# GpSimd's gathers of a chunk: the waits for the preceding chunk's scores and messages are given up, the wait for the sums stays

## The chip, the cores and the metric

One core of one Trainium2 chip. The metric is the device time of one execution in microseconds. The core has five engines that run their own instruction streams and meet at semaphores: TensorE (PE in the profile, its weight loads PEld), VectorE (DVE), ScalarE (ACT), GpSimd (POOL) and SyncE (SP), which issues transfers.

## What is computed

A graph layer followed by a mixture-of-experts layer, each added to its input. The changed code belongs to the graph layer, whose core is:

```python
h_fwd = h @ W_forward.T            # h: 6250 x 256, normalised rows of x
h_rev = h @ W_reverse.T            # 6250 x 64 each
messages = h_fwd[src] * direction[:, 0:1] + h_rev[src] * direction[:, 1:2]   # 200000 edges
scores = leaky_relu(einsum('ef,hf->eh', messages, attn_forward[0]), 0.2)     # 4 heads
exp_scores = exp(scores - scores.max(axis=0))
sum_exp = segment_sum(exp_scores, dst, N)
norm = exp_scores / (sum_exp[dst] + 1e-10)
out = stack([segment_sum(messages * norm[:, hd:hd+1], dst, N) for hd in range(4)], 1)
```

The edges are sorted by `dst`.

## The kernel before

A first stage makes a table of 6272 rows (`node_table`, in HBM): for each node its forward and reverse products and its attention scores, 136 numbers a row. A second stage, the loop over chunks of edges that this case is about, goes through the 200000 edges in 98 chunks (`NCH`) of 16 sets (`K`) of 128 edges. Two chunks make one pass of the hardware loop, and each tensor that is filled ahead has two slots (`RING`), so slot `s` is that of the chunk's parity. Behind it come the expert layer and the last normalisation, which the change does not touch.

What each engine does for chunk `c`:

- GpSimd gathers the table rows of the edges' sources, one indirect transfer of 128 rows (one set) at a time (L259), 14 sets a chunk (`KG`). It works ahead: while the other engines are at chunk `c-1`, it gathers chunk `c`, into the slot that chunk `c-2` has left.
- The other two sets of a chunk (`FILL`), called hot rows, come from TensorE instead: VectorE builds one-hot matrices in two halves (L1070), TensorE multiplies them with a copy of the table that lies on the chip (`fetch`, L979, 34 matmuls a set), ScalarE takes the first third of the result from PSUM (L940), VectorE adds the other two thirds (L1081). While at chunk `c`, TensorE fetches set 1 of chunk `c+1`, then does chunk `c`'s sums, then fetches set 0 of chunk `c+2`.
- VectorE weights the rows by the edge weights (L1005, L1008, L1011), builds the second half of a one-hot matrix (for which TensorE must be through with the fetch before), forms the raw scores (L1025) and the scores (L1027, which raise `score_ready`), the messages (L1038, `msg_ready`) and, from ScalarE's exponentials, the weighted one-hot windows (L1042, `val_ready`). Later it adds TensorE's window sums to the accumulator (L1000, eight instructions, behind a wait for `summed`).
- TensorE multiplies messages with the weighted windows: 32 matmuls for a chunk's sums (`sum_units`, L876), the last of which raises `summed`.
- SyncE loads the next chunk's indices and weights once a chunk's gathers are complete, and the keys of coming hot rows.

GpSimd issues its instructions in the order in which they are written. The only thing that spaces them are its waits. `piece(a, b)` issues the gathers of sets a to b-1. Semaphores count chunks: `msg_ready` at `c-1` means that chunks 0 to `c-2` have their messages, `summed` at `c-1` that chunks 0 to `c-2` are summed, `score_ready` at `c` and `msg_ready` at `c` that the chunk before this one, `c-1`, has its scores and its messages. `settle` raises a semaphore (`turns`) for which nobody waits; the wait written ahead of it stands at that increment.

Of the kernel before, what the change touches and what calls it, by code (L numbers as in the profile page):

```python
# [46 lines left out]
K = 16  # L47
# [52 lines left out]
def after(eng, sem, count):  # L100

    if isinstance(count, int) and count <= 0:
        return
    eng.wait_ge(sem, count)


def settle(eng, turns):


    eng.sem_inc(turns, 1)  # L110
# [107 lines left out]
def stage_edges(nc, tensors, g):  # L218
# [4 lines left out]
    with ExitStack() as edges:  # L223
# [32 lines left out]
        def gather(pool, s, ks, done):  # L256

            for k in ks:
                pool.indirect_dma_start(out=rows[:, s, k, :], out_offset=None, in_=table,  # L259
                                        in_offset=bass.IndirectOffsetOnAxis(ap=index[:, s, 0, k:k + 1], axis=0))\  # L260
                    .then_inc(done, 16)
# [509 lines left out]
        with ExitStack() as ctx:  # L771
# [21 lines left out]
            turns = sem("pool_turns")  # L793
# [5 lines left out]
            msg_ready = sem("messages_ready")  # L799
            hot_ready = sem("hot_ready")  # L800
            max_taken = sem("max_taken")
            score_ready = sem("score_ready")
# [12 lines left out]
            def chunks(eng, begin, step, begun=0):  # L815


                loaded = begin(0)
                for s in range(begun, RING):
                    step(s, s, 0, loaded)  # L820
                with eng.Fori(1, NIT - 2) as it:
                    loaded = begin(it)
                    for s in range(RING):
                        step(it * RING + s, s, it, loaded)
                for it in range(NIT - 2, NIT):
                    loaded = begin(it)
                    for s in range(RING):
                        step(it * RING + s, s, it, loaded)

            def final(c):  # L830

                return isinstance(c, int) and c == NCH - 1
# [5 lines left out]
            def whole(it):  # L838

                return isinstance(it, int) and it == NIT - 1  # L840
# [55 lines left out]
            @block.gpsimd  # L896
            def _(pool):
                def step(c, s, it, _):
                    pool.wait_ge(index_ready[s], 16 * (it + 1))
                    after(pool, msg_ready, c - RING + 1)  # L900
                    settle(pool, turns)
                    begun = EARLY_SETS if isinstance(c, int) and c == EARLY else 0
                    sets = K_LAST if final(c) else K if whole(it) else KG

                    def piece(a, b):
                        gather(pool, s, range(max(a, begun), min(b, sets)), gathered[s])

                    piece(0, 1)
                    after(pool, summed, c - 1)
                    settle(pool, turns)  # L910
                    piece(1, 7)
                    pool.wait_ge(score_ready, c)
                    settle(pool, turns)
                    piece(7, 11)
                    pool.wait_ge(msg_ready, c)
                    settle(pool, turns)
                    piece(11, K)
                pool.wait_ge(prepared, 1)
                chunks(pool, lambda it: None, step, EARLY)

# [1298 lines left out]
```

## Time and profile before

| | us |
|---|---|
| median of 3 runs | 2936.72 (2936.69 to 2939.57) |
| the profiled execution's own time | 2938.83 |
| its span in the trace | 2937.0 |
| busy: PE / PEld / DVE / ACT / POOL | 2194.4 / 1993.9 / 1797.7 / 432.5 / 1630.8 |
| busy POOL in gathers (L259), 1375 of them | 1303.7 |
| idle of POOL just before gathers | 874.8 |

Busy time counts instructions that do work; waits, register and branch instructions are not in it. A matmul's end is modelled in the trace, so a matmul drawn as ended need not be ended. A gather's row on POOL is the time in which its transfer is issued, and its data arrive later. In the timeline views each row is: start us, duration us, engine, line, operation, what it writes and reads, how many instructions are merged in the row, and in brackets the engine's idle time just before it and what ended that. "issue" there means that the profile shows nothing that it waited for, "remote" that a semaphore came whose sender the profile does not name.

### The profile page before, as it was taken

What the parts mean: (1) busy time and instruction counts of PE and PEld (TensorE: products, weight loads), DVE (VectorE), ACT (ScalarE), POOL (GpSimd) and SP (SyncE); (2) the same over time, 40 slices, a digit from 0 to 9 for tenths busy, and PEclk for the clock granted to TensorE, in tenths of its full rate; (3) what the DMA queues carried; (4) which work ended last, traced back from release to release, by engine and by line L of the source; (5) the groups of instructions that cost most, each with busy time, mean ns of one, the idle gap of its engine ahead of it and who ended that gap; (6) DMA issues with size and microseconds to landing.
All of it is one profiled execution on the core that took longest, in us unless ns stands there. A gap on an engine that the chain in (4) does not pass through costs nothing.

```text
span 2937.0 us, 48035 instructions
## 1 busy us (share of the span) xinstructions
PE 2194.4 (75%) x13105; PEld 1993.9 (68%) x13106; DVE 1797.7 (61%) x4481; ACT 432.5 (15%) x1222; POOL 1630.8 (56%) x1750
## 2 busy tenths in 40 slices
PE   6577877778787777787777777777873547999990
PEld 6476767767677676677677677676763446888880
DVE  6666665666565566566556566665654566666666
ACT  4000000000000000000000000000001432434344
POOL 6565565565665555656655656655653555333326
PEclk8789898898898898888888888988985558999995
DMA  5222222222222222222222222222223456556557
GB/s 184 52 53 49 51 51 50 51 52 50 50 53 50 49 51 50 51 48 53 52 48 51 52 50 52 52 50 49 54 48 121 137 174 186 200 187 206 192 170 264
DMA packets 176306, 256.67 MB, mean 87 GB/s; under 512 B 47079, under 2 KB 121000, under 8 KB 176005
## 3 DMA queue, kind: packets, MB, share of 16 engines
q0 software_dynamic: 53696, 121.60, 16.6%
q1 hardware_dynamic: 122564, 134.56, 14.9%
q8 instruction: 17, 0.28, 0.0%
q14 instruction: 29, 0.23, 0.0%
HBM read 218.11 MB, written 38.79 MB: 87 GB/s over the span
## 4 chain that ended last, share of the span: by engine, by line
DVE 29%; issue 26%; PE 24%; another core or an unknown queue 11%; DVEq 7%; DMA 2%; POOL 1%; ACT 1%; SPq 0%; ACTq 0%; POOLq 0%
PE p_hot L979 18%; DVE onehot L1070 5%; DVE shared L1000 3%; DVEq L1726 3%; DVE hot_ex L1042 2%; PE p_win L876 2%; DVE p_part L1008 2%; DVE rows L1081 1%; DVE rows L1005 1%; PE p_y L1894 1%; DVEq L867 1%; DVE p_y L1949 1%; PE p_h L1884 1%; DVE hot L1019 1%
## 5 line engine op out<-in xcount | busy, mean ns | idle before, releaser
L259 POOL DMA_INDIRECT rows<-node_table,index x1375 | 1303.7, 948 | 874.8 <-issue 470.6
L979 PE MATMUL p_hot<-parts,onehot 128*128 128x408 f32 (+1 forms) x6392 | 1410.1, 379 | 364.6 <-issue 192.8
L979 PEld LDWEIGHTS p_hot<-parts,onehot 128*128 128x128 f32 x6392 | 1288.8, 213 | 473.1 <-issue 263.2
L1070 DVE TENSOR_TENSOR onehot<-key,p_dve 128x1152 fp32r<-128x1152 f32 x376 | 473.8, 1281 | 108.8 <-PE p_hot L979 62.0
L1000 DVE TENSOR_TENSOR shared<-shared,p_win 65x64 f32 x784 | 170.9, 218 | 489.1 <-remote 382.0
L876 PE MATMUL p_win<-hot_ex,msg 128*65 128x64 f32 x3136 | 231.5, 228 | 165.1 <-issue 124.6
L876 PEld LDWEIGHTS p_win<-hot_ex,msg 128*65 128x65 f32 x3136 | 207.0, 142 | 196.8 <-issue 195.3
L940 ACT ACTIVATE rows<-p_hot,third 128x136 f32<-128x136 f32 x188 | 70.5, 375 | 1603.9 <-PE p_hot L979 990.5
L1081 DVE SCALAR_TENSOR_TENSOR rows<-p_hot,third,rows 128x136 f32<-128x136 f32 x376 | 134.9, 359 | 243.5 <-issue 192.3
L1735 POOL DMA_INDIRECT expert_rows<-ys,back x104 | 103.1, 992 | 269.4 <-DVE ys L1954 198.4
L1884 PEld LDWEIGHTS p_h<-xt,shared 128*128 128x128 f32 x1664 | 199.9, 194 | 33.9 <-ACT xt L1826 28.6
L1884 PE MATMUL p_h<-xt,shared 128*128 128x128 f32 x1664 | 212.4, 282 | 7.9 <-ACT xt L1826 5.4
L1894 PE MATMUL p_y<-shared,hid_t 128*128 x832 | 199.1, 383 | 9.3 <-DVE hid_t L1921 8.6
L1894 PEld LDWEIGHTS p_y<-shared,hid_t 128*128 128x128 f32 x832 | 151.3, 192 | 26.7 <-issue 9.9
L1305 POOL DMA_INDIRECT dispatched<-xn,slot_i x98 | 100.8, 1028 | 95.3 <-issue 63.4
L1921 DVE TENSOR_SCALAR hid_t<-p_h,shared 128x128 f32<-128x128 f32 x208 | 63.4, 347 | 123.2 <-PE p_y L1894 72.6
L1005 DVE TENSOR_TENSOR rows<-rows,p_attr 128x1088 f32<-128x1088 f32 x98 | 125.7, 1282 | 10.7 <-DMA rows<-node_table,index 5.8
L1008 DVE TENSOR_TENSOR p_part<-rows,p_attr 128x1024 f32<-128x1024 f32 x98 | 119.6, 1221 | 0.0
L1038 DVE TENSOR_TENSOR msg<-rows,p_part 128x1024 f32<-128x1024 f32 x98 | 118.8, 1212 | 0.0
L1042 DVE TENSOR_TENSOR hot_ex<-hot,p_ex 128x1024 f32<-128x1024 bf16 x98 | 118.8, 1212 | 0.0
L931 ACT ACTIVATE p_ex<-score,neg_shift 128x64 f32<-128x64 f32 x98 | 31.2, 318 | 433.5 <-issue 313.3
L1857 ACT ACTIVATE own<-xs,is_first 128x256 f32<-128x256 f32 x104 | 53.1, 510 | 209.4 <-DVE is_first L1932 191.0
(270 smaller groups left out, 1419.0 us busy)
## 6 DMA issues: line engine op xcount, KB each, us to landing
shared<-in_w SPq DMA_DIRECT2D x120, 512.0 KB
rows<-node_table,index POOLq DMA_INDIRECT x1375
xs<-dispatched SPq DMA_DIRECT2D x104, 129.5 KB
key<-hot_keys SPq DMA_DIRECT2D x94, 128.0 KB
shared<-expert_rows SPq DMA_DIRECT2D x12, 896.0 KB, 7.8
token_rows<-in_x SPq DMA_DIRECT2D x7, 896.0 KB
shared<-in_x SPq DMA_DIRECT2D x7, 768.0 KB
out<-shared SPq DMA_DIRECT2D x6, 896.0 KB, 7.3
```

Source lines behind the costliest of these rows:

```text
L259: pool.indirect_dma_start(out=rows[:, s, k, :], out_offset=None, in_=table, in_offset=bass.IndirectOffsetOnAxis(ap=index[:, s, 0, k:k + 1] ...
L876: last = pe.matmul(psum[0:MSG, u * HEADS * W:(u + 1) * HEADS * W], msg[:, k, :], weighted[:, k, :, :].rearrange("p h w -> p (h w)"), start ...
L979: last = pe.matmul(p_hot[:, j, 0:width * ROW], onehot[:, gr, :], parts[:, gr:NT:GP, m, :], start=(gr == 0 and m == 0), stop=(gr == ORDER[- ...
L1000: return dve.tensor_tensor(to, to, psum.rearrange("p (h w) -> p h w", h=HEADS), ALU.add)
L1005: dve.tensor_tensor(rows[:, s, :, 0:COLS], rows[:, s, :, 0:COLS], attr_p[:, 0, :].unsqueeze(2).broadcast_to([P, K, COLS]), ALU.mult)\
L1008: dve.tensor_tensor(p_part[:, :, :], rows[:, s, :, COLS:COLS + HD], attr_p[:, 1, :].unsqueeze(2).broadcast_to([P, K, HD]), ALU.mult)\
L1038: dve.tensor_tensor(msg[:, :, 0:HD], rows[:, s, :, 0:HD], p_part[:, :, :], ALU.add)\
L1042: dve.tensor_tensor(hot_ex[:, :, :, :], hot[:, :, :].unsqueeze(2).broadcast_to([P, K, HEADS, W]), ex_p.unsqueeze(3).broadcast_to([P, K, HE ...
L1070: dve.tensor_tensor(onehot[:, a:b, :], key[:, s, j, :].unsqueeze(1).broadcast_to([P, b - a, P]), group_p[:, a:b].unsqueeze(2).broadcast_to ...
L1081: dve.scalar_tensor_tensor(out=row, in0=p_hot[:, j, m * ROW:(m + 1) * ROW], scalar=third[:, m, ds(f, 1)], in1=row, op0=ALU.mult, op1=ALU.add)\
L1884: last = pe.matmul(p_h[:, u, f // 2, (f % 2) * P:(f % 2 + 1) * P], w1_r[:, r % R5, c, f * P:(f + 1) * P], xt[:, u, c, :], start=(c == 0), ...
L1894: last = pe.matmul(p_y[:, u, 0:D], hid_t[:, u, c, :], w2_sb[:, ds(e, 1), c, :] .rearrange("p a d -> p (a d)"), start=(c == 0), stop=(c == ...
```

## The change

The two waits inside a chunk's gathers and the two `settle` calls behind them are taken out, and the three last pieces become one. The wait for the index, the wait for the messages of chunk `c-2` ahead of the first gather, and the wait for the sums of chunk `c-2` behind it stay as they were.

```diff
                     piece(0, 1)
                     after(pool, summed, c - 1)
                     settle(pool, turns)
-                    piece(1, 7)
-                    pool.wait_ge(score_ready, c)
-                    settle(pool, turns)
-                    piece(7, 11)
-                    pool.wait_ge(msg_ready, c)
-                    settle(pool, turns)
-                    piece(11, K)
+                    piece(1, K)
```

On GpSimd, in the loop over chunks, one even chunk stood like this before; `rows` is the gathered slot, `node_table` the table, and the names in brackets are the semaphores waited for (`window_summed` is `summed`, `messages_ready` is `msg_ready`):

```order
L259 DMA rows<-node_table,index 128x136 [waits messages_ready]
L259 DMA rows<-node_table,index 128x136 [waits window_summed]
L259 DMA rows<-node_table,index 128x136 x5
L259 DMA rows<-node_table,index 128x136 [waits score_ready]
L259 DMA rows<-node_table,index 128x136 x3
L259 DMA rows<-node_table,index 128x136 [waits messages_ready]
L259 DMA rows<-node_table,index 128x136 x2
```

The same chunk of the changed kernel on GpSimd, with the first two gathers of the odd chunk behind it:

```order
L259 DMA rows<-node_table,index 128x136 [waits messages_ready]
L259 DMA rows<-node_table,index 128x136 [waits window_summed]
L259 DMA rows<-node_table,index 128x136 x12
L259 DMA rows<-node_table,index 128x136 [waits index_ready1,messages_ready]
L259 DMA rows<-node_table,index 128x136 [waits window_summed]
```

The 14 gathers are the same and in the same order; the twelve behind the wait for the sums now follow one another without a wait, up to the first gather of the next chunk. No instruction of another engine moves.

## Rows read from the trace of the kernel before

**Rows 1.** The page, busy time, share of the span and instructions of each engine.

```profile
PE 2194.4 (75%) x13105; PEld 1993.9 (68%) x13106; DVE 1797.7 (61%) x4481; ACT 432.5 (15%) x1222; POOL 1630.8 (56%) x1750
```

**Rows 2.** Line L1005 (durations, first and last start), and what ended its waits.

```profile
L1005 DVE TENSOR_TENSOR rows<-rows,p_attr x98: 1275/1281/1290, 92.9 to 2244.3; 128x1088 f32<-128x1088 f32 x98
...
DMA rows<-node_table,index: 5.8, 1
```

**Rows 3.** Line L259, the gathers: idle time before them by releaser (us, times).

```profile
issue: 470.6, 1243
remote: 223.9, 82
DVE score L1027: 179.7, 48
DVE msg L1038: 0.6, 2
```

**Rows 4.** Timeline of POOL, two chunks from 1000 us.

```profile
1003.33 0.95 POOL L259 DMA_INDIRECT rows<-node_table,index  x1 [2.42 <-remote]
...
1011.71 0.94 POOL L259 DMA_INDIRECT rows<-node_table,index  x1 [1.19 <-issue]
...
1020.45 0.95 POOL L259 DMA_INDIRECT rows<-node_table,index  x1 [0.30 <-issue]
1024.23 0.95 POOL L259 DMA_INDIRECT rows<-node_table,index  x1 [2.83 <-remote]
...
1030.48 0.95 POOL L259 DMA_INDIRECT rows<-node_table,index  x1 [0.30 <-issue]
1035.43 1.00 POOL L259 DMA_INDIRECT rows<-node_table,index  x1 [4.00 <-DVE score L1027]
...
1044.24 0.95 POOL L259 DMA_INDIRECT rows<-node_table,index  x1 [0.30 <-issue]
```

**Rows 5.** Timeline of DVE, the same two chunks.

```profile
1002.68 2.67 DVE L1000 TENSOR_TENSOR shared<-shared,p_win 65x64 f32 x8 [5.41 <-remote]
...
1023.58 2.67 DVE L1000 TENSOR_TENSOR shared<-shared,p_win 65x64 f32 x8 [2.10 <-remote]
...
1034.42 0.23 DVE L1027 SCALAR_TENSOR_TENSOR score<-raw 128x64 f32<-128x64 f32 x1
...
1046.97 2.67 DVE L1000 TENSOR_TENSOR shared<-shared,p_win 65x64 f32 x8 [5.80 <-remote]
```

**Rows 6.** Timeline of PE, the sums of the same two chunks.

```profile
1014.47 2.06 PE L876 MATMUL p_win<-hot_ex,msg 128*65 128x64 f32 x31
...
1038.11 2.10 PE L876 MATMUL p_win<-hot_ex,msg 128*65 128x64 f32 x32 [1.12 <-issue]
```

**Rows 7.** Timeline of ACT, hot rows taken from PSUM in the same chunks.

```profile
1017.61 0.38 ACT L940 ACTIVATE rows<-p_hot,third 128x136 f32<-128x136 f32 x1 [6.34 <-remote]
...
1032.81 0.38 ACT L940 ACTIVATE rows<-p_hot,third 128x136 f32<-128x136 f32 x1 [14.59 <-remote]
```

**Rows 8.** Timelines of DVE, POOL, PE and ACT in a chunk with a late restart.

```profile
956.00 2.66 DVE L1000 TENSOR_TENSOR shared<-shared,p_win 65x64 f32 x8 [5.79 <-remote]
...
979.25 2.67 DVE L1000 TENSOR_TENSOR shared<-shared,p_win 65x64 f32 x8 [3.44 <-remote]
...
959.37 0.94 POOL L259 DMA_INDIRECT rows<-node_table,index  x1 [5.14 <-issue]
...
975.63 0.95 POOL L259 DMA_INDIRECT rows<-node_table,index  x1 [0.30 <-issue]
...
967.74 1.75 PE L876 MATMUL p_win<-hot_ex,msg 128*65 128x64 f32 x26
...
971.94 0.37 ACT L940 ACTIVATE rows<-p_hot,third 128x136 f32<-128x136 f32 x1 [7.34 <-issue]
```

**Rows 9.** Timelines of PE and DVE in the last chunk, after the last gather.

```profile
2250.16 3.75 PE L876 MATMUL p_win<-hot_ex,msg 128*65 128x64 f32 x32 [12.73 <-DVE hot_ex L1042]
...
2254.05 2.65 DVE L1000 TENSOR_TENSOR shared<-shared,p_win 65x64 f32 x8 [3.99 <-PE p_win L876]
```

## The prediction, made before the changed kernel had run

> **What bounds the kernel now.** I began with the page's busy line [rows 1]: no engine is full (PE 75%, DVE 61%, POOL 56% of the span), so the time is made of waits, and the stage with the change has to be read by its waits. That stage is the loop over 98 chunks of edges. The view of line L1005, VectorE's first instruction of each chunk, runs from 92.9 to 2244.3 us [rows 2]: 2151.4 us over 97 periods, 22.18 us a chunk, 73% of the span. The reader should see one more thing in that view: L1005 is the instruction that needs the gathered rows, and in the whole run it waited for a gather once, 5.8 us. The rows that GpSimd fetches are never late. What a quicker GpSimd gives cannot come from there.
>
> Next the waits before the gathers [rows 3]. GpSimd idles 179.7 us for the scores in 48 waits (3.74 us each) and 0.6 us for the messages; the waits put down to "remote" (223.9 us) are largely those for the sums, which stay.
>
> Then two neighbouring chunks in the timeline [rows 4]. After the sums GpSimd issues at a fixed pace, 0.95 us a gather and 0.30 us between two. In the first of the two chunks the score wait stretches one gap to 1.19 us (0.89 too much), in the second to 4.00 us (3.70 too much). The chunks alternate like this through the loop.
>
> Last, who ends the chunk. VectorE starts to add the window sums (L1000) at 1002.68, 1023.58 and 1046.97 us [rows 5]. TensorE's records of the 32 sums say that they were done long before: they start at 1014.47 and at 1038.11 and are drawn 2.1 us long (31 records in the first case, a straggler follows) [rows 6], so VectorE starts 9.1 and 8.9 us after TensorE's first sum. In the last chunk, where GpSimd gathers nothing any more, the same 32 sums start at 2250.16 and L1000 follows at 2254.05, 3.89 us later [rows 9]. So TensorE's results are seen late while gathers run. And the moment is tied to the last gather: that one ends at 1020.45+0.95=1021.40 and L1000 starts 2.18 us later; in the next chunk it ends at 1044.24+0.95=1045.19 and L1000 starts 1.78 us later [rows 4, 5]. By this reading a chunk lasts as long as GpSimd's run of 14 gathers, plus what stands around it, and the pause for the scores lies inside that run.
>
> The rows hold a test of it. In one chunk GpSimd restarts late, 3.37 us after the sums (956.00 to 959.37 us), and therefore finds the scores ready; it issues 14 gathers without a pause and ends at 975.63+0.95=976.58 us. L1000 follows at 979.25, 2.67 us after the last gather [rows 8]. The later run has the later sums behind it. Eleven such chunks stand eight apart.
>
> **The change part by part.**
> (1) *The wait for the messages* goes. It cost 0.6 us in all [rows 3]: nothing.
> (2) *The wait for the scores* goes, in every chunk, with its semaphore increment. GpSimd's own idle time that can vanish is 179.7−48×0.30=165.3 us, plus 0.89 us in some 46 chunks of the other sort, 41 us: 206 us at most [rows 3, 4]. This does not follow through one for one, so I build the new chunk instead.
> (3) *The new period.* From L1000 to the first gather behind it: 1002.68 to 1003.33, 0.65 us. Fourteen gathers without a pause: 959.37 to 976.58, 17.21 us. From their end to L1000: 1.78, 2.18 or 2.67 us; I take 2.67, because it belongs to the only row without a score pause [rows 4, 5, 8]. Sum 20.53 us. The late restart comes every eighth chunk: (3.37−0.65)/8=0.34 us a chunk, which I keep in full. 20.87 us against 22.18: 1.31 us gained.
> (4) *Times the chunks.* The first chunks and the last two (which fetch no hot rows) gain nothing by it; I count 93 periods: 122 us. 2938.83 (the profiled execution's own time) −122=2817; that execution lies 2.1 us above the median of the runs, so **2815 us**.
> (5) *What is late next.* The pause has one use. TensorE's hot row for the coming chunk is taken by ScalarE at 1032.81 us [rows 7], 1.38 us after the last gather before the pause ended (1030.48+0.95=1031.43) [rows 4]; VectorE's one-hot build, raw scores and scores wait for the same result. Without the pause it must get through while gathers run. The two rows of that: ScalarE at 1017.61, 3.14 us after TensorE went on to the sums at 1014.47 [rows 6, 7], and 971.94 after 967.74, 4.20 us, in the chunk without a pause [rows 8]. So it comes 0 to about 3.1 us later than now. The scores would end at 1034.65 [rows 5] to 1037.8 us. From there the sums need at least 3.46 us to start (1034.65 to 1038.11 [rows 5, 6]) and 3.89 us to be seen [rows 9]: 1042.0 to 1045.1 us. GpSimd's run would give 1024.23+17.21+2.67=1044.11 us. A delay in the middle (1.6 us) is hidden under the run; the worst costs 1.0 us in every second chunk, 46 us.
>
> Bounds: with 1.78 us behind the last gather and the late restart hidden, 19.64 us a chunk, 236 us gained, 2700 us; with the gain in only one sort of chunk (0.89 us in 46), 2895 us. Likeliest case: 2730 to 2895.
>
> **The rivals.**
> *Same.* The gathers were hidden and stay hidden [rows 2]; the tie of sums to gathers is a coincidence of two things that both follow the scores. For it: in the regular chunks both do start from the scores, so a fixed distance proves little. Against it: the late-restart chunk, and the last chunk's 3.89 us. Time 2937, within 6 us (0.2%, about what a measurement of this kernel can tell from no change). The Trainium skill speaks for this rival ("SBUF — State Buffer", section "SBUF: two separate sides"): a DMA and a compute instruction do not slow each other, and TensorE's ports wait for nobody. By that rule the sums would not move and the time would stay 2937 us; rows 8 and 9 do not fit it.
>
> *Slower: the pause was the gate.* If TensorE's results got out only when the gathers stop, the hot row at L940 would wait for the end of 13 gathers (the 14th, the next chunk's first, still waits for the messages): 1024.23+13×1.25−0.30=1040.18, +1.38=1041.56 instead of 1032.81. The scores would end at 1043.40 and the sums be seen 7.35 us later, at 1050.75 instead of 1046.97: 3.8 us lost. In every second chunk that is 175 us, 3114; if every chunk becomes such a chunk (27.17 us), 3400 us. It decides when the hot row comes more than 4.97 us later than now, since 1034.65+4.97+7.35=1046.97. Against it: 1017.61 and 971.94 came through while gathers ran; for it: 4.20 us is not far from 4.97, and two delays (this one and that of the second hot row) can add up.
>
> *Less.* The chain of hot rows, TensorE to ScalarE to VectorE and back, becomes the bound before GpSimd's run does; then only part of the pause comes back, 2850 to 2930 us.
>
> **How the numbers follow.** Likeliest 0.54, more than it 0.04, less 0.08: faster 0.66. Same 0.12. Slower 0.22, of which 0.07 stays under 2965 us (a small loss, where delays add up in some chunks) and 0.15 lies above, out of the range. Below 2735 us I leave 0.05. Range 2735 to 2965.
>
> **What the profile after would show.** If right: no idle before a gather but 0.30 us and the wait for the sums; L1005's period near 20.9 us; L1000 1.8 to 2.7 us after the last gather; L1005 still not waiting for gathers. If the first rival holds, the gathers end earlier and L1000 does not move. If the second holds, the one-hot build and ScalarE's hot row stand idle far longer than now, and the scores slip. The step most likely to be wrong is (5): a late hot row puts the next fetch, and with it the next chunk's scores, behind.

## The result: 6.0 per cent slower

| | before | after |
|---|---|---|
| median of 4 runs each, us | 2938.14 | 3119.30 (3113.10 to 3122.52) |
| span of the profiled execution, us | 2937.0 | 3115.7 |

The ratio is 1.0602, 95% interval 1.0580 to 1.0623. The forecast was 2815 us, with a range to 2965. The time lies outside it, and near the 3114 us that the rival "the pause was the gate" gave for a loss in every second chunk. Of the runs below, two of e10's six executions fell in a slower state that comes now and then with any kernel; its time is the median of the other four.

In the changed kernel the lines of the loop carry numbers that are lower by 6 (L1005 is L999, L1000 is L994, L940 is L934, L979 is L973, L1070 is L1064, L1081 is L1075). The page's busy line, answering to [rows 1]:

```profile
PE 2200.0 (71%) x13105; PEld 2041.5 (66%) x13106; DVE 1796.7 (58%) x4481; ACT 431.2 (14%) x1222; POOL 1625.0 (52%) x1750
```

No engine has more to do: the busy times stay within some us (the weight loads, 48 us longer, lie beside matmuls), so the loss is waiting. TensorE's granted clock in the loop fell from 0.87 to 0.83, but its busy time there grew by 6.6 us only (1632.2 to 1638.8), and e6 below is faster at 0.72: a slower clock is not the loss. The view of the chunk's first instruction on VectorE, answering to [rows 2]:

```profile
L999 DVE TENSOR_TENSOR rows<-rows,p_attr x98: 1277/1281/1290, 93.9 to 2422.4; 128x1088 f32<-128x1088 f32 x98
...
DMA rows<-node_table,index: 7.1, 1
```

2328.5 us over 97 periods are 24.01 us a chunk, against 22.18 before and 20.87 forecast; 1.83 us times 97 is 177 us of the 179 by which the span grew. The gathers are late for VectorE once, by 7.1 us. GpSimd's idle time before its gathers by releaser, answering to [rows 3]:

```profile
issue: 507.3, 1279
PE p_win L876: 464.9, 83
DVE msg L1032: 83.5, 12
remote: 1.3, 1
```

This is the ledger of the change. The waits given up were worth 180.3 us (179.7 and 0.6). But the wait that stayed, for the sums ("remote" in the view of before), went from 223.9 us in 82 waits to 464.9 us in 83, and 83.5 us in 12 waits are now spent at the head of a chunk, on messages of earlier ones. All four rows together: 874.8 us before, 1057.0 us after, 182 us more. The "issue" row holds, beside the 0.30 us between gathers, a late restart of GpSimd once in eight chunks, 5.14 us in [rows 8] and some 9.4 us now; the view names no wait for it, so GpSimd's gathers are not spaced by its waits alone. GpSimd got rid of a pause of 3.7 us and was made to stand longer elsewhere.

The timelines show what it stands for, first in an ordinary chunk. TensorE's sums, which came in one piece of 31 or 32 in [rows 6], now come singly while GpSimd gathers (columns: start, length, engine, line, operation, tiles, count, idle time before and its releaser; TensorE, GpSimd, VectorE, ScalarE):

```profile
1182.11 0.38 PE L876 MATMUL p_win<-hot_ex,msg 128*65 128x64 f32 x3 [0.43 <-DVE hot_ex L1036]
1183.17 0.22 PE L876 MATMUL p_win<-hot_ex,msg 128*65 128x64 f32 x1 [0.68 <-issue]
...
1188.77 0.27 PE L876 MATMUL p_win<-hot_ex,msg 128*65 128x64 f32 x1 [0.32 <-issue]
1189.48 2.77 PE L876 MATMUL p_win<-hot_ex,msg 128*65 128x64 f32 x23 [0.45 <-issue]
```

```profile
1185.99 0.94 POOL L259 DMA_INDIRECT rows<-node_table,index  x1 [0.30 <-issue]
1193.05 0.94 POOL L259 DMA_INDIRECT rows<-node_table,index  x1 [6.11 <-PE p_win L876]
```

```profile
1174.19 1.28 DVE L999 TENSOR_TENSOR rows<-rows,p_attr 128x1088 f32<-128x1088 f32 x1
...
1178.36 0.23 DVE L1021 SCALAR_TENSOR_TENSOR score<-raw 128x64 f32<-128x64 f32 x1
...
1190.41 0.86 DVE L1075 SCALAR_TENSOR_TENSOR rows<-p_hot,third,rows 128x136 f32<-128x136 f32 x2 [8.57 <-ACT rows L934]
...
1193.58 2.66 DVE L994 TENSOR_TENSOR shared<-shared,p_win 65x64 f32 x8
```

```profile
1189.80 0.37 ACT L934 ACTIVATE rows<-p_hot,third 128x136 f32<-128x136 f32 x1 [10.86 <-remote]
```

The scores come 4.17 us after the chunk's first instruction, as early as before (in about half of the chunks they too are late now, over 6 us behind it, where before none was over 5.4 us). But of the 32 sums only nine come in the 7.4 us up to 1189.48. GpSimd, at the end of a run of 14 gathers, stops at 1185.99+0.94=1186.93 for these very sums; 2.55 us later the other 23 come in one piece, and the second hot row is taken at 1189.80. VectorE adds the sums (L994) 6.65 us after the last gather. Before, that distance was 1.7 to 2.9 us in every chunk; now it is 3.9 to 6.9 us, and over 6.2 us in 76 of the 92 chunks between the first and the last few. A run of 17.2 us and 6.7 us behind it make up the 24 us of a chunk.

The second stretch follows a late restart and is of the rarer sort: it ends with GpSimd stopped for messages, which comes 12 times in the run.

```profile
1036.16 1.21 PE L876 MATMUL p_win<-hot_ex,msg 128*65 128x64 f32 x17 [0.39 <-DVE hot_ex L1036]
...
1040.07 0.27 PE L876 MATMUL p_win<-hot_ex,msg 128*65 128x64 f32 x1 [1.13 <-issue]
1040.76 0.26 PE L876 MATMUL p_win<-hot_ex,msg 128*65 128x64 f32 x1 [0.42 <-issue]
1041.49 0.26 PE L876 MATMUL p_win<-hot_ex,msg 128*65 128x64 f32 x1 [0.46 <-issue]
...
1046.38 0.82 PE L876 MATMUL p_win<-hot_ex,msg 128*65 128x64 f32 x6 [1.02 <-issue]
1049.33 11.65 PE L973 MATMUL p_hot<-parts,onehot 128*128 128x408 f32 x52 [2.12 <-DVE onehot L1064]
1067.65 4.38 PE L973 MATMUL p_hot<-parts,onehot 128*128 128x272 f32 x16 [6.68 <-DVE onehot L1064]
```

"issue" here means that TensorE waited for no operand and no engine that the profile shows; that its next instruction was not there yet is my reading, which no view shows. The first 17 sums take 1.21 us; after that they come singly or in pairs, most of them 0.7 to 1.4 us apart, and only when GpSimd has stopped do the last six run together. The sums of the next chunk fall into a stop of GpSimd, but for one gather, and come in one piece again (at 1071.87, in 2.05 us). GpSimd in the same stretch:

```profile
1042.88 0.94 POOL L259 DMA_INDIRECT rows<-node_table,index  x1 [0.30 <-issue]
1048.00 0.94 POOL L259 DMA_INDIRECT rows<-node_table,index  x1 [4.17 <-PE p_win L876]
...
1062.97 0.94 POOL L259 DMA_INDIRECT rows<-node_table,index  x1 [0.30 <-issue]
1071.20 0.94 POOL L259 DMA_INDIRECT rows<-node_table,index  x1 [7.29 <-DVE msg L1032]
```

VectorE and ScalarE, answering to [rows 5, 7]:

```profile
1055.02 1.35 DVE L1064 TENSOR_TENSOR onehot<-key,p_dve 128x1152 fp32r<-128x1152 f32 x1 [2.03 <-PE p_hot L973]
...
1066.37 1.22 DVE L1064 TENSOR_TENSOR onehot<-key,p_dve 128x1024 fp32r<-128x1024 f32 x1 [7.43 <-remote]
...
1068.09 0.23 DVE L1021 SCALAR_TENSOR_TENSOR score<-raw 128x64 f32<-128x64 f32 x1
```

```profile
1066.48 0.37 ACT L934 ACTIVATE rows<-p_hot,third 128x136 f32<-128x136 f32 x1 [19.34 <-remote]
```

TensorE's 52 matmuls are drawn to 1060.98, but VectorE's second half of the one-hot tile and ScalarE's hot row, which both wait for the fetch that the first 34 of them make, start at 1066.37 and 1066.48. GpSimd's last gather ends at 1062.97+0.94=1063.91; the result is taken 2.57 us after that. So a circle closes in such a chunk: the hot row comes through when GpSimd stops, the scores (1068.09) and the messages follow the hot row, and GpSimd, which has run on to the next chunk's first gather, stops until those messages are there.

Summed over the run it is in the view of groups (busy time and mean of one, then idle time before and its releasers): TensorE before the sums, VectorE before the hot rows that it completes, ScalarE before the hot row.

```profile
L876 PE MATMUL p_win<-hot_ex,msg 128*65 128x64 f32 x3136 | 373.6, 287 | 486.6 <-issue 440.4 <-DVE hot_ex L1036 30.4 <-remote 15.5
...
L1075 DVE SCALAR_TENSOR_TENSOR rows<-p_hot,third,rows 128x136 f32<-128x136 f32 x376 | 135.0, 359 | 641.3 <-ACT rows L934 608.5 <-DVE rows L1075 12.6 <-issue 0.2
...
L934 ACT ACTIVATE rows<-p_hot,third 128x136 f32<-128x136 f32 x188 | 70.2, 373 | 1994.2 <-remote 1594.5 <-PE p_hot L973 327.6 <-issue 72.0
```

Before, the three idled 165.1, 243.5 and 1603.9 us.

### The profile page after: what moved, and what is told of

Same layout as the page of the kernel before. It is cut to its first block, busy times and chain, and to the rows that moved or that the text cites. A ratio compares the mean times of both kernels' runs of the same rounds, so it can differ in the third digit from the quotient of the medians.

```text
span 3115.7 us, 47795 instructions
## 1 busy us (share of the span) xinstructions
PE 2200.0 (71%) x13105; PEld 2041.5 (66%) x13106; DVE 1796.7 (58%) x4481; ACT 431.2 (14%) x1222; POOL 1625.0 (52%) x1750
## 3 DMA queue, kind: packets, MB, share of 16 engines
q0 software_dynamic: 53696, 121.60, 15.8%
## 4 chain that ended last, share of the span: by engine, by line
PE 28%; another core or an unknown queue 28%; issue 20%; DVE 15%; DVEq 5%; DMA 2%; ACT 1%; POOL 1%; ACTq 0%; SPq 0%; POOLq 0%
PE p_hot L973 21%; PE p_win L876 4%; DVEq L1720 3%; DVE onehot L1064 2%; PE p_y L1888 1%; DVE p_y L1943 1%; PE p_h L1878 1%; DVEq L867 1%; DVE second L1923 1%; DVE p_part L1002 1%; DVE hid_t L1915 1%; DVE back L1928 1%; ACT rows L934 1%; DVE rows L1075 1%
## 5 line engine op out<-in xcount | busy, mean ns | idle before, releaser
L259 POOL DMA_INDIRECT rows<-node_table,index x1375 | 1298.5, 944 | 1057.0 <-issue 507.3
L973 PE MATMUL p_hot<-parts,onehot 128*128 128x408 f32 (+1 forms) x6392 | 1278.6, 361 | 213.4 <-DVE onehot L1064 129.2
L973 PEld LDWEIGHTS p_hot<-parts,onehot 128*128 128x128 f32 x6392 | 1217.3, 202 | 235.0 <-DVE onehot L1064 143.2
L876 PE MATMUL p_win<-hot_ex,msg 128*65 128x64 f32 x3136 | 373.6, 287 | 486.6 <-issue 440.4
L876 PEld LDWEIGHTS p_win<-hot_ex,msg 128*65 128x65 f32 x3136 | 329.4, 199 | 563.1 <-issue 561.6
L1064 DVE TENSOR_TENSOR onehot<-key,p_dve 128x1152 fp32r<-128x1152 f32 x376 | 474.7, 1283 | 260.2 <-remote 194.6
L1075 DVE SCALAR_TENSOR_TENSOR rows<-p_hot,third,rows 128x136 f32<-128x136 f32 x376 | 135.0, 359 | 641.3 <-ACT rows L934 608.5
L934 ACT ACTIVATE rows<-p_hot,third 128x136 f32<-128x136 f32 x188 | 70.2, 373 | 1994.2 <-remote 1594.5
L994 DVE TENSOR_TENSOR shared<-shared,p_win 65x64 f32 x784 | 170.4, 217 | 116.6 <-remote 15.9
L999 DVE TENSOR_TENSOR rows<-rows,p_attr 128x1088 f32<-128x1088 f32 x98 | 125.8, 1284 | 11.9 <-DMA rows<-node_table,index 7.1
L1833 ACT ACTIVATE hid_t<-p_h,shared 128x128 f32<-128x128 f32 x208 | 65.0, 363 | 13.9 <-PE p_h L1878 7.4
```

What stands on the lines that cost most here:

```text
L876: last = pe.matmul(psum[0:MSG, u * HEADS * W:(u + 1) * HEADS * W], msg[:, k, :], weighted[:, k, :, :].rearrange("p h w -> p (h w)"), start ...
L973: last = pe.matmul(p_hot[:, j, 0:width * ROW], onehot[:, gr, :], parts[:, gr:NT:GP, m, :], start=(gr == 0 and m == 0), stop=(gr == ORDER[- ...
L994: return dve.tensor_tensor(to, to, psum.rearrange("p (h w) -> p h w", h=HEADS), ALU.add)
L999: dve.tensor_tensor(rows[:, s, :, 0:COLS], rows[:, s, :, 0:COLS], attr_p[:, 0, :].unsqueeze(2).broadcast_to([P, K, COLS]), ALU.mult)\
L1064: dve.tensor_tensor(onehot[:, a:b, :], key[:, s, j, :].unsqueeze(1).broadcast_to([P, b - a, P]), group_p[:, a:b].unsqueeze(2).broadcast_to ...
L1075: dve.scalar_tensor_tensor(out=row, in0=p_hot[:, j, m * ROW:(m + 1) * ROW], scalar=third[:, m, ds(f, 1)], in1=row, op0=ALU.mult, op1=ALU.add)\
```

## The experiments

All times stand beside runs of the kernel before on the same chip (2934 to 2996 us from chip to chip); ratios are against those, with their 95% intervals. "Period" is the spacing of VectorE's first instructions of a chunk.

**One wait at a time.** The first two runs take one of the two waits away and keep the other.

```
# e1_score_kept                      # e2_msg_kept
  piece(1, 7)                          piece(1, 11)
  pool.wait_ge(score_ready, c)         pool.wait_ge(msg_ready, c)
  settle(pool, turns)                  settle(pool, turns)
  piece(7, K)                          piece(11, K)
```

> Only the wait for the messages is given up, the wait for the scores stays. Theory A (the pause for the scores is the gate: TensorE's finished results are seen late while GpSimd issues gathers, and come through in the pause): the time of before, 2937 us within 0.3%. Theory B (each wait carries a part, GpSimd has to be kept in step with VectorE at several points): a part of the loss of 181 us, 2980 to 3060 us.

> Only the wait for the scores is given up, the wait for the messages behind the eleventh gather stays. In the changed kernel the messages come so late that this wait would bind. Theory A: a pause four gathers (5 us) later lets the results through 5 us later than the pause for the scores, the loss is a good part of 181 us: 2990 to 3100 us. Theory B: the messages' wait keeps step, 2940 to 2990 us.

e1 took 2936.16 us, ratio 0.9996 (0.9980 to 1.0012), period 22.09 us: the wait for the messages is worth nothing, as step (1) said. e2 took 3074.23 us, ratio 1.0436 (1.0396 to 1.0477). The loss belongs to the pause for the scores; a later pause for the messages makes up a quarter of it.

**Another pause in its place.** Is it the scores that GpSimd must wait for, or must it only stop? e3 stops after the 7th gather for the first set of hot rows, e8 after the 10th for the second set as well. e5 stops for nothing but its own gathers. All three keep the wait for the sums.

```
# e3_hot_wait                                       # e5_own_pause
  piece(1, 7)                                         piece(1, 7)
  if coming(s, it, 0, 0):                             if not begun:
      pool.wait_ge(hot_rows, fill_of(s, it) + 1)          pool.wait_ge(gathered[s], 16 * (KG * it + 7))
      settle(pool, turns)                                 settle(pool, turns)
  piece(7, K)                                         piece(7, K)
# e8_hot_wait2: as e3, and after the 10th gather the same wait with + 2
```

> In place of the waits for scores and messages GpSimd waits, at the same place behind the seventh gather, for TensorE's first hot row of the chunk that it is gathering, the very result that the pause would let through. Theory A: the pause ends some 2 us sooner in every second chunk (1032.7 in place of 1034.7 us in the trace of before), GpSimd's run ends sooner and the sums with it: 2850 to 2930 us. Theory B: another thing than the scores is waited for, step is lost, 2960 to 3120 us.

> The changed kernel with one wait put in after the 7th gather of a chunk: GpSimd waits there until its own first seven gathers have landed, which depends on no other engine; scores, messages and hot rows are not waited for. Theory A (any pause of GpSimd lets TensorE's work through): the time comes most of the way back from 3119 us, to 2930 to 3000 us, near the 2954 us of the run that paused for the hot rows. Theory B (it is the order between GpSimd and the others that counts, so a pause that is tied to nothing only delays GpSimd): 3119 us or more, up to 3119 plus 93 pauses of about 2 us, 3300 us.

> The changed kernel with two waits put in: after the 7th gather of a chunk for the first set of hot rows, after the 10th for the second set. Theory A (pauses that end when TensorE's fetch is through pay for themselves): the long chunks of 25 to 27 us that were left with one such wait (2954 us) go, 2850 to 2930 us. Rival (each further wait only takes GpSimd's time, 2 to 4 us in a chunk where it bites): 2960 to 3100 us.

e3: 2954.47 us, 1.0056 (1.0036 to 1.0077). e5: 2951.15 us, 1.0042 (1.0015 to 1.0068). e8: 3043.05 us, 1.0359 (1.0318 to 1.0401). e5 answers the question: a pause of about 2.4 us tied to no other engine brings back nearly all of the loss. What I expected of e3 (a gain) and of e8 failed: in e8, as its rival said, the further wait only took GpSimd's time, whose idle time before gathers is 984.0 us, against 894.3 in e3, about what the span is longer (3041.0 and 2957.0 us).

**Who issues, and in which form.** e4 and e7 replace each gather by a plain copy of 128 table rows of the same size, issued by SyncE and by GpSimd. e12 makes two half-row copies of it, so that GpSimd has no break. e18 keeps the indirect gather, but always of rows 0 to 127 in order. All four leave the gathered rows out.

```
# e4_sync_copies: on SyncE, behind the same waits (both ahead of the first copy); no gather on GpSimd in the loop
  sp.dma_start(rows[:, s, k, :], table[k * P:(k + 1) * P, :]).then_inc(copied_sp[s], 16)
# e7_pool_plain
  pool.dma_start(rows[:, s, k, :], table[k * P:(k + 1) * P, :]).then_inc(done, 16)
# e12_pool_twice
  for a, z in ((0, ROW // 2), (ROW // 2, ROW)):
      pool.dma_start(rows[:, s, k, a:z], table[k * P:(k + 1) * P, a:z]).then_inc(done, 16)
  ...   # the waits for gathers count twice as far
# e18_row_order
  in_offset=bass.IndirectOffsetOnAxis(ap=own_row[:, 0:1], axis=0)   # own_row[p] = p
```

> The changed kernel with SyncE issuing the transfers in GpSimd's place behind the same waits, as plain copies of 128 table rows (the gathered rows are left out, the bytes, the tiles and the number of transfers stay). Theory A, GpSimd's issuing is what holds TensorE up: L1000's wait and the hot rows' waits vanish, a chunk falls to 16 to 19 us, 2400 to 2650 us. Theory C (the transfers themselves, their bytes and their landing, hold TensorE up, whoever issues them): within 3% of the changed kernel, 3030 to 3200 us.

> The changed kernel with each of GpSimd's gathers replaced by a plain copy of 128 table rows of the same size, issued by GpSimd behind the same waits (the gathered rows are left out: fixed rows of the table are copied). Theory A (what holds TensorE up is GpSimd's making of the descriptors in its software queue): if a plain copy is issued in the same 0.95 us the time stays at 3050 to 3150 us. Rival (it is the indirect addressing of the gather that holds the others up): 2250 to 2600 us, near the 2279 us of the copies that SyncE issued.

> The changed kernel with each gather replaced by two plain copies of half a row each, issued by GpSimd (the gathered rows are left out: fixed rows of the table are copied), so that GpSimd issues for 28 times 0.53 us, 14.9 us a chunk, nearly as long as 14 gathers take (17.5 us) and without the long pauses of the run with 14 copies. Theory of the indirect form (only the gathers hold TensorE up): GpSimd's copies and TensorE's 14.6 us of matmuls lie side by side, a period of 16 to 18 us, 2300 to 2500 us. Rival (any steady issuing of GpSimd holds TensorE up; the 2276 us came from the pauses): results are seen late and sums crawl again, a period of 21 us or more, 2830 to 3150 us.

> The changed kernel with every gather of the loop given one fixed list of rows, 0 to 127 in order (the gathered rows are left out): still 14 indirect gathers a chunk by GpSimd, but the addresses are as regular as those of the plain copies. If the indirect form itself holds TensorE up: the time stays within 2 per cent of the changed kernel, 3060 to 3180 us, about 1.04 to 1.08 of the time before. If it is the scattered addresses of the rows: TensorE comes through and GpSimd's pace of 17.5 us and a wait sets the period, 2500 to 2800 us, 0.85 to 0.93.

| run | us | ratio |
|---|---|---|
| e4_sync_copies | 2278.63 | 0.7755 (0.7731 to 0.7778) |
| e7_pool_plain | 2275.63 | 0.7745 (0.7721 to 0.7770) |
| e12_pool_twice | 2287.70 | 0.7654 (0.7639 to 0.7670) |
| e18_row_order | 3144.54 | 1.0721 (1.0696 to 1.0747) |

e4 refuted that the bytes are to blame. e7 refuted my own wording, that GpSimd's software queue is: the same packets go through that queue (53696, 121.60 MB, in both pages). One doubt was left, since GpSimd stood still for 8 of 15.4 us in e7; e12 takes it away. Its timeline of GpSimd, then of TensorE:

```profile
999.80 40.65 POOL L260 DMA_DIRECT2D rows<-node_table  x77
```

```profile
1005.88 2.10 PE L875 MATMUL p_win<-hot_ex,msg 128*65 128x64 f32 x32 [0.39 <-DVE hot_ex L1035]
1008.40 12.43 PE L972 MATMUL p_hot<-parts,onehot 128*128 128x408 f32 x68 [0.42 <-DVE onehot L1063]
1021.31 2.10 PE L875 MATMUL p_win<-hot_ex,msg 128*65 128x64 f32 x32 [0.48 <-DVE hot_ex L1035]
```

GpSimd issues 77 copies in 40.65 us without a gap, and TensorE goes from fetch to sums and back with half a microsecond between them, 100 matmuls in 15.4 us. With 14 gathers a chunk the shortest period of any run is 21.0 us, and that with 66 matmuls (e6). In e18, at last, regular addresses bring nothing back; its groups show the same crawl as the changed kernel:

```profile
L261 POOL DMA_INDIRECT rows<-node_table,own_row x1375 | 1299.9, 945 | 1056.1 <-issue 499.0 <-PE p_win L880 480.2 <-DVE msg L1036 73.8
...
L880 PE MATMUL p_win<-hot_ex,msg 128*65 128x64 f32 x3136 | 384.0, 291 | 504.4 <-issue 441.0 <-DVE hot_ex L1040 45.8 <-remote 17.4
```

So it is the indirect form of the transfer that holds TensorE up, not its bytes, addresses, queue or GpSimd being busy. (e4 and e12 came out faster than any time named for them.)

**How many instructions.** e6 leaves out the low parts of the table in the fetch, 34 matmuls instead of 68.

```
-                        for m in range(2):
+                        for m in range(1):
...
-                                             stop=(gr == ORDER[-1] and m == 1))
+                                             stop=(gr == ORDER[-1]))
```

> The changed kernel with TensorE's fetch of a hot row cut from 68 to 34 matmuls (the low parts of the table are left out, so the hot rows lack them). Theory A1 (what reaches TensorE while GpSimd issues gathers is a number of instructions: some 60 go through, each one after that takes 0.7 to 1.4 us): with 66 instead of 100 matmuls per fetch and sums nearly nothing is left to crawl, the period falls from 24.0 to GpSimd's own 20 to 21 us, and the time to 2750 to 2850 us. Theory A2 (results are seen some 3 to 9 us late by time, whatever their number): the work of TensorE falls by some 7 us a fetch but the delays stay; 2950 to 3100 us.

2823.37 us, ratio 0.9617 (0.9586 to 0.9648), with the view of the chunk's first instruction:

```profile
L999 DVE TENSOR_TENSOR rows<-rows,p_attr x98: 1276/1279/1291, 93.0 to 2130.6; 128x1088 f32<-128x1088 f32 x98
```

The period is 21.01 us. With 66 matmuls a chunk instead of 100 the crawl of the sums is gone, VectorE adds them 2.9 us after the last gather, and GpSimd's run sets the pace: this period is the one that my steps (3) and (4) described (20.87 us, 2815 us). TensorE is still held up, now in the fetch (361.1 us of "issue" before its matmuls, against 82.9 in the changed kernel), but it has the time for it. The fetch has fewer instructions and takes less time as well, and e6 does not tell which of the two counts.

**How many pauses, where and how long.** e9 to e11 leave one pause a chunk; e13 to e17 have only pauses tied to a gather's landing. To wait for one gather, it counts on a semaphore of its own, which VectorE waits for too; SyncE's wait before an index load is moved to VectorE's first multiplication. The wait for messages at the head of a chunk stays in all eight; that for the sums is left in e11 only.

```
# e9_score_only                   # e10_pause_only              # e11_sums_mid
  piece(0, 7)                       piece(0, 7)                   piece(0, 7)
  pool.wait_ge(score_ready, c)      (the wait of e5)              after(pool, summed, c - 1)
  settle(pool, turns)               piece(7, K)                   settle(pool, turns)
  piece(7, K)                                                     piece(7, K)

# e15_four_short
  .then_inc(marked[s] if k in (2, 5, 9, 12) else done, 16)
...
  def seen(pool, s, it, j, begun):
      j = max(j, len([k for k in (2, 5, 9, 12) if k < begun]))
      pool.wait_ge(marked[s], 16 * (4 * it + j))
      settle(pool, turns)
...
  piece(0, 4); seen 1; piece(4, 7); seen 2; piece(7, 11); seen 3; piece(11, 14); seen 4
# e13: (6, 13) after 7, 14;  e14: (5, 12) after 7, 14;  e16: (3, 8, 12) after 5, 10, 14
# e17: (1, 4, 7, 10, 12) after 3, 6, 9, 12, 14
```

> The kernel before with only one of its three pauses inside a chunk's gathers: the wait for the scores after the 7th gather stays, the waits for the sums and for the messages go. Theory A1 (TensorE needs GpSimd's pauses; about 60 of its instructions come through after each, and a fetch and its sums are 100) makes two pauses a chunk necessary: the sums crawl as in the changed kernel, 2990 to 3150 us. Rival (one pause of some 4 us in the middle of the gathers is enough, and the wait for the sums only paced GpSimd): GpSimd saves the 224 us in which it waited for sums, the period falls to 17.5 plus 4 us or less, and the time to 2800 to 2900 us.

> No wait of GpSimd for scores, messages or sums; the only pause inside a chunk's gathers is the one for its own first seven gathers (2.4 us, after the 7th). Theory A1 (two pauses a chunk are needed): 3000 to 3200 us, at or above the changed kernel. Rival (a short pause in the middle is enough): GpSimd is the bound with 17.5 plus 2.4 us a chunk, 2730 to 2830 us.

> The changed kernel with its one wait, that for the sums, moved from behind the first gather to behind the seventh. Theory A (what counts is that GpSimd pauses, and one pause a chunk leaves runs of 14 gathers wherever it stands): 3050 to 3180 us, near the changed kernel's 3119 us. Rival (the place counts: a pause in the middle of the gathers comes when the sums or the hot row stand at the door): 2850 to 2960 us.

> No wait of GpSimd for sums, scores or messages; two pauses a chunk, after the 7th and after the 14th gather, each until the gather issued last has landed (about 2.4 us of idle time, tied to no other engine). Theory A1 (two pauses a chunk let TensorE's 100 instructions through): GpSimd sets the pace with 17.5 plus twice 2.1 us and 0.3 us for the late restarts, 22.0 us a chunk, which is 0.99 to 1.00 of the time before. Rival (pauses must also come when TensorE's results stand at the door): as the run with one such pause, 1.03 to 1.08.

> As the run with two pauses, but each only until the gather before the last two has landed, about 1.1 us of idle time in place of 2.4 us (0.3 us of it is there between any two gathers). If the mere break is what counts: 17.5 plus twice 0.8 and 0.3 us, 19.4 us a chunk, 0.90 to 0.94 of the time before. If a break of this length is too short for TensorE: sums crawl as in the changed kernel, 1.02 to 1.08.

> Four short pauses of about 1.1 us a chunk, after the 4th, 7th, 11th and 14th gather, and no other wait inside the gathers. If the mere break counts: 17.5 plus four times 0.8 and 0.3 us, 21.0 us a chunk, 0.95 to 0.97 of the time before. If a break of this length is too short: 1.05 to 1.10, as GpSimd is slower on top of the crawl.

> Three short pauses of about 1.1 us a chunk, after the 5th, 10th and 14th gather, and no other wait inside the gathers. If the number of pauses decides and a chunk's 100 instructions of TensorE come through in three portions: 17.5 plus three times 0.8 and 0.3 us, 20.2 us a chunk, 0.91 to 0.95 of the time before. If four are needed: between the run with two (1.17) and the run with four (0.96), 1.00 to 1.10.

> Five short pauses of about 1.1 us a chunk, after the 3rd, 6th, 9th, 12th and 14th gather. If GpSimd already sets the pace with four: 0.8 us more a chunk, 22.3 us, 0.98 to 1.00 of the time before. If TensorE still waits with four: 21 to 21.6 us a chunk, 0.94 to 0.96.

| run | pauses in a chunk | us | ratio |
|---|---|---|---|
| e9_score_only | one, for the scores | 3449.15 | 1.1536 (1.1512 to 1.1560) |
| e10_pause_only | one of 2.4 us | 3115.72 | 1.0418 (1.0393 to 1.0444) |
| e11_sums_mid | one, for the sums | 3116.52 | 1.0414 (1.0365 to 1.0463) |
| e14_two_short | two of 1.1 us | 3511.70 | 1.1731 (1.1702 to 1.1760) |
| e13_two_long | two of 2.4 us | 2943.23 | 0.9831 (0.9809 to 0.9853) |
| e16_three_short | three of 1.1 us | 3167.43 | 1.0565 (1.0544 to 1.0585) |
| **e15_four_short** | four of 1.1 us | 2884.78 | **0.9634 (0.9610 to 0.9658)** |
| e17_five_short | five of 1.1 us | 2965.10 | 0.9899 (0.9876 to 0.9921) |

One pause is too little wherever it stands (e10, e11). e9 was far worse than I expected. Its timelines of TensorE, VectorE and GpSimd show why:

```profile
1030.80 2.10 PE L876 MATMUL p_win<-hot_ex,msg 128*65 128x64 f32 x32 [1.12 <-issue]
```

```profile
1046.03 2.67 DVE L994 TENSOR_TENSOR shared<-shared,p_win 65x64 f32 x8 [12.18 <-remote]
```

```profile
1044.40 0.94 POOL L259 DMA_INDIRECT rows<-node_table,index  x1 [0.30 <-issue]
1055.06 0.94 POOL L259 DMA_INDIRECT rows<-node_table,index  x1 [9.72 <-DVE score L1021]
```

The 32 sums start at 1030.80 and VectorE adds them 15.2 us later, 0.69 us after the end of the last of GpSimd's 14 gathers without a break. Only then does VectorE come to the scores for which GpSimd waits 9.72 us: the gathers hold up the very result that ends the pause.

The short pauses, tied to nothing, have a best number. With two, GpSimd's releasers read (first e14, then e15, then what VectorE's first instruction waited for in e17):

```profile
DVE msg L1044: 799.1, 76
...
DMA rows<-node_table,index: 95.5, 81
```

```profile
DMA rows<-node_table,index: 267.9, 226
DVE msg L1050: 13.7, 1
```

```profile
L1020 DVE TENSOR_TENSOR rows<-rows,p_attr 128x1088 f32<-128x1088 f32 x98 | 126.1, 1287 | 540.5 <-DMA rows<-node_table,index 537.1 <-issue 3.4
```

With two short pauses GpSimd is stopped 76 times for messages, 10.5 us each, because TensorE's results come late: in one chunk a fetch drawn to 1021.1 is taken at 1031.1, 2.3 us after the last gather. That is the circle again, now in most chunks, and slower than either of my expectations of e14. With four it is stopped once. With five VectorE waits 537.1 us for the gathers themselves: GpSimd is now the bound, and the fifth pause only delays it. (In e15 that wait is 177.1 us, in the kernel before 5.8 [rows 2].)

e15 beats both kernels. No run has SyncE's moved wait alone, so the gain over the kernel before belongs to the pauses, the wait for the sums that is gone and this move together; the order among e13 to e17, which share both, belongs to the pauses. Its page and the view of the first instruction, period 21.56 us:

```profile
PE 2099.7 (73%) x13105; PEld 1949.5 (68%) x13106; DVE 1796.3 (62%) x4481; ACT 431.8 (15%) x1222; POOL 1623.8 (56%) x1750
```

```profile
L1017 DVE TENSOR_TENSOR rows<-rows,p_attr x98: 1276/1287/1290, 94.9 to 2186.1; 128x1088 f32<-128x1088 f32 x98
```

## Why the prediction was wrong

- **Step (1)**, messages cost nothing: right (e1, 0.9996).
- **Step (2)**, GpSimd's idle time for scores goes, and that alone proves nothing: right. The releaser is gone from the view, and GpSimd's idle time before gathers is still 182 us more in all.
- **Step (5) failed, and with it one term of step (3).** Step (5) let the hot row come at most 3.1 us later without the pause, from two rows in which one had come through under gathers ([rows 6 to 8]), hid a middle delay of 1.6 us under GpSimd's run, and took 3.89 us for the sums, from the one chunk without gathers [rows 9]. So step (3) kept 2.67 us from the last gather to L1000. In its place the runs show a mean of 6.3 us (6.65 in the ordinary chunk above), because sums and the second hot row came through only when the run had ended; behind a late restart the first hot row did too, 2.57 us after its end (1066.48). I took the delay for a fixed time per result, while it depends on how much TensorE has to bring through between two breaks (e6).
- **The rest of steps (3) and (4)** was sound: GpSimd's run of 14 gathers took the 17.2 us that they say. The period was 24.01 us for 20.87 mainly by that one term; e6, in which TensorE has a third less to get through, ran at 21.01 us and 2823 us.
- **The reading of rows 5, 8 and 9 was right, and its use wrong.** I had seen that sums become visible about 2 us after the last gather and concluded that a shorter run of gathers ends the chunk sooner. If TensorE's results are sure to come through only when GpSimd stops, a pause inside the run is not a mere delay but a second chance for them, and e1 and e5 bear that out.
- **The rival "the pause was the gate"** named the mechanism, results that get out only when the gathers stop, and 3114 us (measured 3119). Its path is the rarer one: it closed the circle over the messages at the next chunk's first gather, where GpSimd stops in 12 chunks (83.5 us), while it stops for the sums, one gather later, in 83 (464.9 us). So the near hit is partly luck: the rival put 3.8 us on every second chunk, while the periods, which alternated between some 21.1 and 22.9 us with every eighth at 25.1, are now 23.6 us throughout with every eighth at 27.6. I gave the slower cases 0.22.
- **The rule cited for "same"** (the Trainium skill, "SBUF — State Buffer", section "SBUF: two separate sides") that transfers and compute do not slow each other agrees with the plain copies: in e12 TensorE's 68 matmuls take 12.43 us under unbroken copies. The time forecast from it did not come out for indirect gathers (e18 and the changed kernel); whether they hold TensorE up at the ports of which the page speaks, or elsewhere, no run shows.

What stays open is the path inside the chip by which an indirect gather keeps TensorE's matmuls and results back, and what makes GpSimd restart late once in eight chunks; no view shows either. Nor is it settled why two pauses of 1.1 us (1.173) do worse than one of 2.4 us (1.042).

## What to carry to other kernels

A wait that protects no data may still do work: before it is removed, look at what comes through on the *other* engines while its engine stands still. When an engine shows "issue" idle time in single instructions, look for what another engine is issuing at that moment, and test it by changing the form of that work (here a plain copy for a gather) before changing the order. If pauses are needed, tie them to the engine's own progress and find their number by trial: four of 1.1 us gave 0.963, three 1.057 and five 0.990, while a pause tied to a result that the work itself holds back made a circle (1.154).

## What the runs showed of the hardware

- While GpSimd issued indirect gathers (0.94 us each, 0.30 us between), TensorE's matmuls came singly, most of them 0.7 to 1.4 us apart, after the first few of a chunk's sums (3 in one chunk, 17 in another), and in e9 the 32 sums, drawn 2.10 us long, were taken 15.2 us after their start, against 3.89 us with no gathers [rows 9].
- Plain copies of the same or twice the number through the same queue did nothing of the sort: 0.53 us each, 77 in a row, TensorE undisturbed. The stage of the gathers took 15.4 us a chunk with them, against 22.18 us before: three tenths of this loop are the price of the indirect form, its longer issue included.
- With four breaks of some 1.1 us in 14 gathers the loop ran at 21.56 us a chunk, and the sums came in one piece in nearly every chunk; with two it was the slowest kernel of all.
